# Combining the results of eight experts: loads, sums and inverse roots regrouped in a kernel of twelve stages

## What is computed

```python
def _rmsnorm(x, w):
    var = jnp.mean(x * x, axis=-1, keepdims=True)
    return w * (x * jax.lax.rsqrt(var + EPS_NORM))
...
src = x + _gqa(x, ...)
src = _rmsnorm(src, norm1_w)
src = src + _moe(src, gate_w, w1, w2)     # the sum of two experts' weighted results for each token
return _rmsnorm(src, norm2_w)
...
x = x + 0.5 * _L3_ffn_ref(...)
```

## Time and profile before

| | us |
|---|---|
| median of 3 runs (3924.92, 3925.31, 3944.54) | 3925.31 |
| the profiled execution's own time | 3935.15 |
| its span, first to last instruction | 3933.4 |
| combining of l3f1, first load issued to last addition | 50.67 |
| combining of l3f2, the same | 50.53 |
| all 32 scaling instructions (L2549) of l3f2c, busy | 9.1 |
| DVE busy in one combining | 28.93 |
| ACT busy in one combining | 10.22 |
| POOL busy in one combining | 27.26 |

### The profile page before, as it was taken

The page is one execution under the profiler, slowest core; times in us unless marked ns, Lnnn a source line. Parts: engine busy times, 40 slices in busy tenths (PEclk is TensorE's granted clock), DMA queues, the critical chain, the costliest instruction groups (busy, mean ns, idle before and its releaser), DMA issues. The chain is left out here.

```text
span 3933.4 us, 70148 instructions
## 1 busy us (share of the span) xinstructions
PE 2708.0 (69%) x24900; PEld 1753.0 (45%) x24900; DVE 2212.2 (56%) x5951; ACT 1409.4 (36%) x2942; POOL 1920.1 (49%) x2400
## 2 busy tenths in 40 slices
PE   3339937633797454799967999471688875999471
PEld 2228824422686142555544555361233332555361
DVE  6752347567333444367743675414599997675413
ACT  1112204211121313346532565132667661566131
POOL 4767740077386212257742111566588784111565
PEclk7769968677899687889987899585799997899586
DMA  9108941110488442000000100132112110010132
GB/s 338 47 6 203 226 111 35 46 65 17 107 230 198 175 135 115 9 16 17 15 7 12 20 17 11 53 88 57 76 54 86 52 78 12 18 19 11 52 86 77
DMA packets 231098, 294.78 MB, mean 75 GB/s; under 512 B 36614, under 2 KB 187527, under 8 KB 224656
## 3 DMA queue, kind: packets, MB, share of 16 engines
q1 hardware_dynamic: 176912, 246.21, 20.4%
q0 software_dynamic: 47616, 39.44, 5.0%
q10 hardware_dynamic: 6272, 5.24, 0.5%
HBM read 182.43 MB, written 107.12 MB: 74 GB/s over the span
## 5 line engine op out<-in xcount | busy, mean ns | idle before, releaser
L3378 PE MATMUL l3am_y<-l3am_hc,ident 128*128 128x512 f32 x512 | 280.4, 631 | 95.6 <-DVE l3am_hc L3287 95.5
L3067 POOL TENSOR_TENSOR l3am_db<-l3am_du,l3am_bs 128x512 f32<-128x512 f32 x256 | 317.9, 1272 | 43.6 <-DVE l3am_hh L3279 43.6
L3279 DVE TENSOR_TENSOR_SCAN l3am_hh<-l3am_dA,l3am_db 128x512 f32<-128x512 f32 x256 | 301.4, 1214 | 48.2 <-ACT l3am_dA L3187 47.0
L777 POOL TENSOR_TENSOR l2a_pT<-l2a_pT,kept 128x512 int32<-128x512 int32 x192 | 241.6, 1272 | 116.5 <-ACT l2a_pT L992 115.8
L879 DVE CUSTOM_DVE_ANT_0 l2a_junk<-l2a_s,addend 128x256 f32<-128x256 f32 x512 | 187.4, 421 | 82.0 <-PE l2a_s L1106 68.5
L2460 POOL DMA_INDIRECT l0f_table<-l0f2e_y,l0f2e_idx x128 | 178.8, 1397 | 103.7 <-DVE l0f2e_idx L2432 57.6
L2054 POOL DMA_INDIRECT l0f_rows<-l0f1r_row,l0f1r_idx x160 | 172.7, 1079 | 94.0 <-issue 94.0
L2460 POOL DMA_INDIRECT l0f_table<-l0f1e_y,l0f1e_idx x128 | 179.7, 1404 | 67.0 <-issue 32.2
L872 DVE TENSOR_REDUCE l3f2a_mx<-l3f2a_s 128x2 f32<-128x512 f32 x256 | 165.6, 686 | 67.5 <-PE l3f2a_s L1106 66.2
L872 DVE TENSOR_REDUCE l3f1a_mx<-l3f1a_s 128x2 f32<-128x512 f32 x256 | 165.6, 686 | 67.2 <-PE l3f1a_s L1106 66.0
L3378 PEld LDWEIGHTS l3am_y<-l3am_hc,ident 128*128 128x128 f32 x512 | 91.2, 194 | 227.8 <-DVE l3am_hc L3287 176.7
(11 more groups left out here) (749 smaller groups left out, 7120.4 us busy)
## 6 DMA issues: line engine op xcount, KB each, us to landing
l3am_bs<-l3a_b SPq DMA_DIRECT2D x32, 1024.0 KB, 4.7
l0f1m_w<-in_L_ffn_expert_w SPq DMA_DIRECT2D x64, 384.0 KB, 3.2
l0f2m_w<-in_L_ffn_expert_w SPq DMA_DIRECT2D x64, 384.0 KB, 3.2
l0f_rows<-blank SPq DMA_DIRECT2D x8, 1930.0 KB, 21.6
l0f1m_w<-in_L_ffn_expert_w SPq DMA_DIRECT2D x64, 192.0 KB, 3.6
l0f2m_w<-in_L_ffn_expert_w SPq DMA_DIRECT2D x64, 192.0 KB, 3.6
l1a_top<-l1a_kernel SPq DMA_DIRECT2D x12, 1024.0 KB, 11.9
l3f_rows<-blank SPq DMA_DIRECT2D x8, 1440.0 KB, 11.1
```

Of the source, the lines that this page charges most:

```text
L777: self.nc.gpsimd.tensor_tensor(t, t, self.kept[:, f // 8 % 2, :].unsqueeze(1).to_broadcast([P, 2, 2 * P]), ALU.mult).then_inc(self.cut_g, 1)
L3067: G.tensor_tensor(db[j][n % 2][:, :], du[j][k % 2][:, :], bs[s // QUARTER][:, s % QUARTER, :], ALU.mult).then_inc(db_ready[j], 1)
L3279: V.tensor_tensor_scan(hh[j][n % 2][:, :], dA[j][n % 2][:, :], db[j][n % 2][:, :], 0.0, ALU.mult, ALU.add).then_inc(h_ready, 1)
L3378: T.matmul(yb[j][:, :], c.ident[:, :], hc[j][n % 2][:, :], start=(s == 0), stop=(s == N - 1)).then_inc(summed, 1)
```

## The change

The function `combine` loses its part with a norm, and a new function `combine_normed` takes its place in the stages l3f1 and l3f2. It does the same arithmetic in another order:

- The two results of a token are stored side by side, in rows 2n and 2n + 1 of `l3f_tables`. This is the edit in `route`.
- SP issues eight loads of 512 KB, one for each group and each into a buffer of its own, with the weight row after the first. Each run of consecutive bytes in device memory is 1024 bytes in place of 512.
- DVE makes the sums of all groups first, and writes them into `src` itself.
- There are two solvers of 128x16 numbers, one for each half of the groups, in place of eight uses of solvers of 128x4.
- ACT multiplies each tile by its inverse root, in place in `src`. DVE multiplies a whole group by the weight row and then adds half of it to x.

```diff
 (route)
-                    nc.vector.scalar_tensor_tensor(row[u][:, :, D + E:R], second, float(TABLE),
-                                                   token.to_broadcast([P, TPG, E]), ALU.mult, ALU.add).then_inc(steps, 1)
+                    nc.vector.scalar_tensor_tensor(row[u][:, :, D + E:R], token.to_broadcast([P, TPG, E]), 2.0, second,
+                                                   ALU.mult, ALU.add).then_inc(steps, 1)
 (combine: its part with source, norm and w is taken out; in its place, called by gqa_moe:)
+def combine_normed(nc, c, name, m, source, norm, w):
+    with Phase(nc, name) as ph:
+        HALF = GROUPS // 2
+        both = [ph.sb(f"both{k}", [P, TPG, 2, D]) for k in range(GROUPS)]
+        s01 = [ph.sb(f"s01{i}", [P, TPG, D]) for i in range(2)]
+        sq, ss = ph.sb("sq", [P, 2, TPG, D]), [ph.sb(f"ss{h}", [P, HALF * TPG]) for h in range(2)]
+        nw = ph.sb("nw", [P, D])
+        rms = [Rsqrt(ph, c, f"rms{h}", HALF * TPG) for h in range(2)]
...
+        @block.sync
+        def _(sp):
+            for k in range(GROUPS):
+                sp.dma_start(both[k][:, :, :, :], m.all_tables[2 * GT * k:2 * GT * (k + 1), :].rearrange(
+                    "(t p j) d -> p t j d", p=P, j=2)).then_inc(loaded[k], 16)
+                if k == 0:
+                    sp.dma_start(nw[:, :], w[norm][0, :].partition_broadcast(P)).then_inc(weights, 16)
+        @block.scalar
+        def _(a):
+            for k in range(GROUPS):
+                a.wait_ge(summed, k + 1)
+                if k >= 2:
+                    a.wait_ge(squared, k - 1)
+                for t in range(TPG):
+                    n = TPG * (k % HALF) + t
+                    ins = nc.scalar.activation(sq[:, k % 2, t, :], source[:, TPG * k + t, :], ACT.Square,
+                                               accum_out=ss[k // HALF][:, n:n + 1])
+                ins.then_inc(squared, 1)
+            for k in range(GROUPS):
+                if k % HALF == 0:
+                    a.wait_ge(rms[k // HALF].solved, 1)
+                    a.wait_ge(squared, GROUPS)
+                for t in range(TPG):
+                    n = TPG * (k % HALF) + t
+                    ins = nc.scalar.activation(source[:, TPG * k + t, :], source[:, TPG * k + t, :], ACT.Copy,
+                                               scale=rms[k // HALF].y[:, n:n + 1])
+                ins.then_inc(scaled, 1)
+        @block.gpsimd
+        def _(g):
+            for h in range(2):
+                rms[h].pool(g, 0)
+        @block.vector
+        def _(v):
+            def root(h):
+                v.wait_ge(squared, HALF * (h + 1))
+                rms[h].dve(v, ss[h][:, :], 0, 1.0 / D, RMS_EPS)
+            def apply(k):
+                v.wait_ge(scaled, k + 1)
+                xt, st = tiles4(c.x, k), tiles4(source, k)
+                nc.vector.tensor_tensor(st, st, nw[:, :].unsqueeze(1).to_broadcast([P, TPG, D]), ALU.mult).then_inc(weighed, 1)
+                v.wait_ge(weighed, k + 1)
+                nc.vector.scalar_tensor_tensor(out=xt, in0=st, scalar=0.5, in1=xt, op0=ALU.mult, op1=ALU.add)
+            for k in range(GROUPS):
+                v.wait_ge(loaded[k], 16)
+                if k >= 2:
+                    v.wait_ge(summed, k - 1)
+                nc.vector.tensor_tensor(s01[k % 2][:, :, :], both[k][:, :, 0, :], both[k][:, :, 1, :], ALU.add).then_inc(added, 1)
+                v.wait_ge(added, k + 1)
+                st = tiles4(source, k)
+                nc.vector.tensor_tensor(st, st, s01[k % 2][:, :, :], ALU.add).then_inc(summed, 1)
+                if k == HALF + 1:
+                    root(0)
+            v.wait_ge(weights, 16)
+            apply(0)
+            apply(1)
+            root(1)
+            for k in range(2, GROUPS):
+                apply(k)
```

More of the change, by code:

```diff
@@ L2466, in _, with combine @@
                 g.wait_ge(t, 16 * (units * A // len(added)))
-def combine(nc, c, name, tables, source=None, norm=None, w=None):
+def combine(nc, c, name, tables):
     with Phase(nc, name) as ph:
@@ L2473, in combine @@
         acc = [ph.sb(f"acc{i}", [P, TABLES, GT]) for i in range(DEPTH)]
-        s01, out = [ph.sb(f"s01{i}", [P, GT]) for i in range(2)], ph.sb("out", [P, GT])
+        s01 = [ph.sb(f"s01{i}", [P, GT]) for i in range(2)]
         loaded = [ph.sem(f"loaded{i}") for i in range(DEPTH)]
[L2476 to L2482, removed]
+        free, applied = ph.sem("free"), ph.sem("applied")
         block = ph.block()
@@ L2486, in _ @@
         def _(sp):
-            if source is not None:
-                sp.dma_start(nw[:, :], w[norm][0, :].partition_broadcast(P)).then_inc(weights, 16)
             def load(i, u):
@@ L2503, in _ @@
                     load(i, u)
[L2505 to L2520, removed]
         @block.vector
         def _(v):
-            if source is not None:
-                v.wait_ge(weights, 16)
             def sums(i, u, k):
                 if not isinstance(k, int) or k >= 2:
-                    v.wait_ge(applied if source is None else scaled, k - 1)
+                    v.wait_ge(applied, k - 1)
                 v.wait_ge(loaded[u], 16 * TABLES * (i + 1))
@@ L2532, in sums @@
                 v.wait_ge(free, k + 1)
-                if source is not None:
-                    s3 = s01[u % 2][:, :].rearrange("p (t d) -> p t d", t=TPG)
-                    nc.vector.tensor_tensor(s3, s3, tiles4(source, k), ALU.add).then_inc(steps, 1)
             def body(i, u, k):
@@ L2539, in body @@
                 xt = tiles4(c.x, k)
[L2540 to L2553, removed]
+                nc.vector.scalar_tensor_tensor(out=xt, in0=s3, scalar=0.5, in1=xt, op0=ALU.mult, op1=ALU.add
                                                ).then_inc(applied, 1)
[L2556 to L2559, removed]
             def step(at):
-                if at(1):
-                    root(*at(1))
                 body(*at(0))
@@ L2569, in _ @@
             sums(0, 1, 1)
-            root(0, 0, 0)
             stream(v, GROUPS, DEPTH, step)
+def combine_normed(nc, c, name, m, source, norm, w):
[6 more added lines that the diff above has]
+        rms = [Rsqrt(ph, c, f"rms{h}", HALF * TPG) for h in range(2)]
+        loaded = [ph.sem(f"loaded{k}") for k in range(GROUPS)]
+        weights, added, summed, squared, scaled, weighed = (
+            ph.sem(s) for s in ("weights", "added", "summed", "squared", "scaled", "weighed"))
+        block = ph.block()
+        @block.sync
[56 more added lines that the diff above has]
+                apply(k)
@@ L2593, in gqa_moe @@
             experts(nc, c, name + "e", w, m, mats, 8, 2, 2, 2, False, sub=P, U=10, unroll=20)
-        combine(nc, c, name + "c", m.tables, source=src, norm="L3_ffn_norm2_w", w=w)
+        combine_normed(nc, c, name + "c", m, src, "L3_ffn_norm2_w", w)
 def grouped_attention(nc, c, name, w, src):
```

## The result

The changed kernel takes 3901.85 us (median of 6 runs, 3894.54 to 3910.05), the kernel before 3927.6 (6 runs, 3916.12 to 3944.54). The ratio is 0.9933, with a 95% interval of 0.9909 to 0.9957, so 0.4 to 0.9% faster. In a second set of runs it was 3897.38 against 3926.67, a ratio of 0.9928 (0.9904 to 0.9952). The prediction was 3900.7.

The account below looks back on a forecast made before the run. No engine bounds the whole kernel; stages follow each other behind barriers, and combinings wait on turns between engines. Shortening both combinings to 38.3 us takes 24.6 off the 3925.3 us median, giving 3900.7 us, range 3888 to 3911.

Parts of the forecast that it names:

- What bounds the combining: Combining windows, 101.2 us together: no engine full; DVE, ACT and POOL hand work round, about 5.1 us a turn per group.
- First load: Start of a combining: without the weight row in front, the first sum starts 3.7 us after the first DMA issue.
- The other seven loads: Loads after the first: 1.50 us a group, plus 1.2 first-gap excess and 2.2 weight row; last group there at 17.6.
- Sums ending at 19.45: DVE's sums: loads set the pace, the first guess takes 0.6, groups 6 and 7 run back to back to 19.45.
- First Newton: POOL's first root: starts at 16.8, four instructions slowed beside DVE, eight at 0.30, done at 21.9 us.
- Applying: DVE behind the roots: one product with the broadcast weight row and one addition, 1.33 us a group.
- Stalls of 3.8: DVE idle some 3.8 us before the first product and again before the fifth, waiting for Newton and ACT's scaling.
- Length 38.3: Each combining, first DMA issue to last addition: 38.3 us instead of 50.53 and 50.67, together 24.6 us less.
- The rival of slow loads: Combining's loads: longer runs bring no speed, last group at 19.6 instead of 17.6, total 3904.7 us; chance 0.14.
- The rival of better loads: Combining's loads: weight row hides, first gap's excess vanishes, last group at 14.2, total 3892.7 us; chance 0.14.
- Slower scatters: Experts' result writes: neighbouring places disturb each other, each +0.1 us costs 16 us; at +0.3, 3949 us; chance 0.03.
- The POOL contention: POOL's Newton instructions: about 0.67 us apart beside DVE's large instructions, 0.30 apart with DVE idle.

## Why the prediction was right

The whole time came out 1.2 us from the forecast. That is luck in part, since the six runs spread over 15 us and the kernel before has moved from 3925.3 to 3927.6; what tests the mechanism are the windows and the terms of the sum.

- **What bounds the combining: turns between engines.** Right, but the prediction did not say how near POOL alone stands behind them. In the kernel before each of POOL's sequences starts where the last one ends, or 0.43 us later:

```profile
3897.14 0.24 POOL L157 TENSOR_TENSOR l3f2c_rms_t<-l3f2c_rms_y 128x4 f32<-128x4 f32 x1 [0.43 <-DVE l3f2c_rms_y L147]
...
3902.16 0.20 POOL L157 TENSOR_TENSOR l3f2c_rms_t<-l3f2c_rms_y 128x4 f32<-128x4 f32 x1
...
3907.37 0.24 POOL L157 TENSOR_TENSOR l3f2c_rms_t<-l3f2c_rms_y 128x4 f32<-128x4 f32 x1 [0.43 <-DVE l3f2c_rms_y L147]
```

So POOL waits for another engine for 0.43 us in the 10.2 of two groups. It counts as busy for 27.3 us only, yet its chain of 96 instructions, each waiting for the one before, takes 38.9 us from the first start to the last end. That is why a shorter way round the other engines alone gains next to nothing: all of the change with eight roots has a chain of 38.2 us and is no faster, and the loads alone brought 0.2 to 0.6 us. What pays is that one Newton sequence serves four groups, and that is possible because all sums are made first. The two belong together; the runs do not price the second alone.
- **First load, 3.7.** Measured 4.1 and 3.9.
- **The other seven loads, 17.6 with 1.2 for a long first gap and 2.2 for the weight row.** The rate was right (1.50 a group, 352 GB/s). The weight row costs 2.0 and 2.4, as taken. The 1.2 was wrong: with the weight row last the first gap is 1.50 like the others. This is the term that was mis-sized; with the first load 0.2 to 0.4 later, group 5's first sum starts at 13.6 and 13.8, not 14.6. Why l0f1c has a long first gap was not tried.
- **Sums ending at 19.45.** Measured 18.2 and 18.4, for the same reason, and because DVE was held up by the first guess for 0.4 us (3875.14 to 3875.55) where the sum has 0.8 (16.0 to 16.8).
- **First Newton, 5.1, done at 21.9; second 5.0, done at 31.6.** Measured 5.25 each (3875.73 to 3880.98, 3885.71 to 3890.97, l3f2c), done at 21.1 and 31.1. Four instructions in step with DVE, then eight: right. I costed 128x16 at nothing; it is 0.33 in place of 0.31 from start to start.
- **ACT's first scaling 1.3.** Measured 1.38 and 1.31 from its start to DVE's product.
- **Applying, 1.33 a group, broadcast operand included.** Measured 1.33.
- **Stalls of 3.8.** Measured 4.08 and 4.01.
- **Length 38.3, 24.6 us off in all.** Measured 37.6 and 37.8, 25.8 off.

The rival of slow loads had its mechanism (512 bytes would have cost 1.5 to 2.4 us) but not its case. Its 2.0 us also mixed two prices, for it took 2.6 for the weight row where the forecast took 2.2; with 2.2 it is 1.6. The rival of better loads was right about the first gap and wrong about the weight row. It was priced too high besides: it lets DVE set the pace with 1.33 us a group, but loads of 1.50 are slower than that whatever the first gap is. With the gap at 1.50 the combining took 35.7 us, not 33.9. Slower scatters did not come: they start 1.28 us apart. The POOL contention was as priced; the Trainium skill ("GPSIMD Engine Reference", Key points) says that POOL shares its SBUF interfaces with DVE and that instructions of DVE with two SBUF inputs contend with it. The trace agrees: POOL's instructions take up to 0.66 us beside such instructions and 0.20 to 0.22 with DVE idle.

## What to carry to other kernels

Where several engines hand small pieces round and none is full, count the turns and ask what one turn can serve; here the same twelve instructions on 128x16 cost nearly as much as on 128x4. A low busy share can hide a chain of small dependent instructions that fills the time, as POOL's did. Then look at the engine that stands idle behind such a chain: DVE was waiting for Newton steps on POOL, and one large root on DVE took off another 4.3 to 4.5 us, of which some 3 by estimate are due to the engine. Moving work to an idle engine (ScalarE's scaling) brought nothing here, where its first result stands in the chain. A small load that is needed late belongs behind the large ones that are waited for; here that was worth 1.9 to 2.2 us a combining.

## What the runs showed that I had not expected

- A load of 64 KB that copies one row of 512 bytes to 128 partitions held up the stream by 2.0 and 2.4 us; 0.7 to 0.8 MB would pass in that time at 350 GB/s. In l3f2c of the changed kernel, the windows of one microsecond from 3863 on, between the first and the second group, moved 102, 114, 283 and 387 GB/s.
- Splitting the root in two halves, so that the first is early, made the combining 1.2 to 1.7 us longer than one root for all.
- Two executions of one kernel differed by 21 us outside the changed stage; of that, 13.8 us in one attention stage, where the mean granted clock was 0.86 in one and 0.89 in the other.
